# One factor moved out of the inverse sums, one copy moved to another engine, and a new order for the drain of an attention and feed-forward kernel

## Chip, cores and metric

The kernel runs on one core of a Trainium2 chip. The metric is the device time of one execution in microseconds (us). TensorE is PE, VectorE DVE, ScalarE ACT, GpSimd POOL, and SyncE (SP) issues the transfers. Instructions of one engine run in order; engines wait for each other only through semaphores.

## What is computed

```python
def layer(x, weight_qkv, out_w, out_b, W_r, W_k, W_v, mu_r, mu_k):     # x: 4 x 2048 x 256
    x = x + layernorm(attention(layernorm(x)))
    x = x + layernorm(ffn(layernorm(x)))

def attention(x):
    q, k, v = split(x @ weight_qkv)        # two column bands of x in fp16, the rest in fp32
    s = softmax((q / sqrt(256)) @ k.T)
    return (s @ v) @ out_w.T + out_b

def ffn(x):
    x_prev = x shifted by one row, zero in the first row of each batch
    xr, xk = mu_r * x + (1 - mu_r) * x_prev, mu_k * x + (1 - mu_k) * x_prev
    return sigmoid(xr @ W_r.T) * (square(relu(xk @ W_k.T)) @ W_v.T)
```

The layer norms have no learned factors and an epsilon of 1e-5.

## The kernel before

The 8192 rows are worked on in H = 32 halves of 256 rows, 8 for each of the 4 batches (PER = 8, RT = 2 tiles of 128 rows in a half). A half has 8 score tiles of 128x512, and one score tile is a slot: SLOTS = 256. The loops of all five engines run over the slots, and a table of offsets says in which slot after its own first one a half gets each operation: values from slot 23, the attention rows at 33, their normalization at 34, the turned sum and the differences at 45, the mixes at 48 and 50, receptance at 53, keys at 54, feed at 58, the gated rows at 59, the store at 65. So about nine halves are under way at a time, and where several operations fall in a slot, the order of the if statements is their order on that engine. Every product is made in split precision: a value is stored as a high fp16 part and a low part (value minus high), and three matmuls replace one. PE multiplies, ACT makes the high parts, exponents and most normalizations, DVE and POOL the low parts.

The next batch is loaded, normalized, split and transposed while the current one is computed (PREP, every 12 slots, during halves 10 to 15 and 18 to 23, and in the start-up).

What the change touches:

- inverse_sums(h), DVE: the reciprocal of the row sums (L1019), then its product with top[OUT], the largest magnitude of the folded projection weights, by which these weights had been divided (L1021). attention(h) uses the product as the factor of the projected rows (L1030) and adds bias_row.
- att_rsqrt(h), POOL: variance plus eps (L508), power -0.5 (L512), and the shift for attention_norm(h) on ACT (L765).
- scales(), POOL, once, in slot 17: the small factors that depend on the weights.
- mix_in_sum(h), differences(h), carry(h), POOL, slot 45. The first adds the two transposed parts into xt (L568), which has 257 columns; the second subtracts neighbouring columns (L577); carry copies the last column to column 0 of the other xt buffer, 128x2 elements, or clears it at the end of a batch (L589, L587). It waits for the mixes of the half before.
- ACT in slots of the kind of 46: receptance (L792) and gate_norm (L811); then in the next slot attended_high (y_hi, L695) and squares (L799 to L804).

Other names in the rows: probs and p_lo (L994, L1010) are the scores copied from PSUM and the low part of the exponents; q_lo (L985) and y_lo (L1014) are low parts of the query and of the attended values; rvar and rrstd (L524, L526) belong to res_rsqrt; pvar, prstd and xs (L467, L470, L919) to the preparation of a batch; res (L552 on POOL, L1097 on DVE) is add_attention; xm_lo (L595, L1112) is split_low.

After the last slot each engine runs a list of calls written out by hand, the drain, in which helpers of the same name exist on DVE and on POOL (split_low, squares_low, add_attention, differences, finish) and on DVE and ACT (attention_norm, gate_norm), so that the list decides who does it. In the drain the transposition for the mix goes through PE (turn_mix_in, L1365) instead of a transfer.

Of the kernel before, what the change touches and what calls it, by code (L numbers as in the profile page):

```python
# [8 lines left out]
ALU = mybir.AluOpType  # L9
# [3 lines left out]
P = 128  # L13
BLK = 512
EPS = 1e-5
# [3 lines left out]
def sandwich(nc, x, w_qkv, out_w, out_b, w_r, w_k, w_v, mu_r, mu_k, out):  # L19
# [51 lines left out]
    DIFF = 45  # L71
    MIX = (48, 50)
# [23 lines left out]
    MIX_LEFT = H - 6  # L96
# [9 lines left out]
    with ctx:  # L106
# [19 lines left out]
        eps = sb("eps", [P, RT])  # L126
# [144 lines left out]
        scales_made = sem("scales_made"); feed_part_made = sem("feed_part_made"); sum_inverted = sem("sum_inverted")  # L271
# [67 lines left out]
        def _(sp):  # L339
# [112 lines left out]
        def _(pool):  # L452
            pool.memset(ident[:, :], 0.0).then_inc(ident_zero, 1)
            pool.memset(minus_half[:, :], -0.5).then_inc(consts_made, 1)
            pool.memset(eps[:, :], EPS).then_inc(consts_made, 1)
# [6 lines left out]
            pool.wait_ge(consts_made, 3)  # L462
# [9 lines left out]
            def scales():  # L472
# [6 lines left out]
                pool.wait_ge(inv_top_made, 1)  # L479
                pool.tensor_scalar(mix_shrink[:, 0:1], top[:, MU:MU + 1], 2.0 ** -MIX_EXP, 0.0, ALU.mult,  # L480
# [99 lines left out]
            def carry(h):  # L580
                if h >= TURN_LEFT:
                    pool.wait_ge(xt_made, h + 1)
                if h >= 1:
                    pool.wait_ge(mixed_made[0], h * HALVES)
                    pool.wait_ge(mixed_made[1], h * HALVES)
                if (h + 1) % PER == 0:
                    pool.memset(xt[:, (h + 1) % 2, :, 0:1], 0.0).then_inc(carried, 1)  # L587
                else:
                    pool.tensor_copy(xt[:, (h + 1) % 2, :, 0:1], xt[:, h % 2, :, ROWS:ROWS + 1]).then_inc(carried, 1)  # L589

# [33 lines left out]
            for k in range(SLOTS):  # L624
# [14 lines left out]
                if (h := at(k, DIFF)) is not None:  # L639
                    mix_in_sum(h)  # L640
                    differences(h)
                    carry(h)
# [9 lines left out]
            carry(H - 5)  # L652
            att_rsqrt(H - 4, H - 3)
            add_attention(H - 4)
            split_low(H - 5, 1)
            res_rsqrt(H - 4)
            split_low(H - 5, 0)
            att_rsqrt(H - 3, H - 2)
            carry(H - 4)
            differences(H - 4)  # L660
            gate_rsqrt(H - 7, 0)
            finish(H - 7)
            gate_rsqrt(H - 6, H - 6)
            add_attention(H - 3)
            att_rsqrt(H - 2, 0)
            res_rsqrt(H - 3)
            finish(H - 6)
            split_low(H - 4, 1)
            carry(H - 3)
            differences(H - 3)  # L670
            res_rsqrt(H - 2)
            gate_rsqrt(H - 5, 0)
            split_low(H - 3, 1)
            finish(H - 5)
            carry(H - 2)
            squares_low(H - 4)
            split_low(H - 3, 0)
            att_rsqrt(H - 1, 0)
            split_low(H - 2, 1)
# [6 lines left out]
            gate_rsqrt(H - 3, H - 5)  # L686
            finish(H - 3)
            gate_rsqrt(H - 2, H - 4)
# [4 lines left out]
        def _(act):  # L693
# [87 lines left out]

            def split_high(h, i):
# [43 lines left out]
            for k in range(SLOTS):  # L826
# [30 lines left out]

            mix_in_out(H - 5)
            exponents(H - 1, 1)
            split_high(H - 6, 0)  # L860
            split_high(H - 6, 1)
            probs_high(H - 1, 0)
            attention_norm(H - 4, H - 3)
            split_high(H - 5, 1)
            probs_high(H - 1, 1)
            attended_high(H - 3)
            split_high(H - 5, 0)
# [652 lines left out]
```

## Time and profile before

| | |
|---|---|
| three runs | 830.95, 833.72, 833.16 us; median 833.16 |
| profiled execution | 831.39 us |
| its span, first to last instruction | 829.6 us |
| busy share of PE, DVE, ACT, POOL | 94%, 92%, 61%, 58% |
| first score matmul, last slot, last feed | 23.5, 750, 820.9 us |

In a row of the timeline the first figure is the start in us from the first instruction, the second the duration, then engine, line of the kernel, operation, output and inputs with their shapes, and in brackets the idle time of the engine before it with what ended it. Durations of neighbouring instructions on an engine overlap a little, matmuls above all; from start to start one of 256 columns takes 0.109 us and one of 512 columns 0.215 us.

### The profile page before, as it was taken

The page shows a single profiled execution, that of the slowest core. Times are in us where ns is not written, and L with a number is a line of the kernel's source. Part 1 is how long each engine was busy: PE and PEld are TensorE (multiplying, and loading weights), DVE is VectorE, ACT ScalarE, POOL GpSimd, SP SyncE. Part 2 cuts the span into 40 slices and gives each one's busy share as a digit, 9 for nine tenths or more (in the row PEclk, how much of TensorE's full clock was granted, in tenths as well). Part 3 has the DMA queues.
Part 4 walks back from the last instruction along what each step waited for, and adds up shares of the span by engine and source line. Part 5 has one row for each costly group of instructions (what it writes and reads, how often), then busy time and mean ns, then how long its engine had stood idle before and what let it go on. Part 6 is the DMA issues. An engine that isn't in the chain of part 4 may idle for free.

```text
span 829.6 us, 16266 instructions
## 1 busy us (share of the span) xinstructions
PE 782.6 (94%) x5765; PEld 568.3 (69%) x5765; DVE 759.6 (92%) x1822; ACT 510.0 (61%) x631; POOL 479.8 (58%) x692
## 2 busy tenths in 40 slices
PE   4879999999999998999999998999999999998983
PEld 3436677777767775777776775777777777777872
DVE  5698989999999999999999999999999999899895
ACT  3375555676666665667656666666766667665453
POOL 2210255577656566576655766656776576567674
PEclk9999999999999999999999999999999999999998
DMA  7565777587757585756676755747767465458301
GB/s 183 115 152 109 152 170 142 122 160 141 155 87 160 124 175 118 146 132 119 158 127 152 151 132 119 160 90 160 140 140 141 105 113 115 108 122 185 83 26 52
DMA packets 365090, 108.69 MB, mean 131 GB/s; under 512 B 338768, under 2 KB 364752, under 8 KB 365008
## 3 DMA queue, kind: packets, MB, share of 16 engines
q1 hardware_dynamic: 365008, 107.64, 62.4%
q8 instruction: 46, 0.75, 0.4%
q14 instruction: 36, 0.29, 0.1%
HBM read 18.75 MB, written 8.39 MB: 33 GB/s over the span
## 4 chain that ended last, share of the span: by engine, by line
PE 61%; DVE 32%; issue 4%; POOL 1%; DMA 1%; SPq 1%; ACT 0%; DVEq 0%; POOLq 0%
DVE p_lo L1010 7%; DVE probs L994 6%; PE S L1308 5%; PE S L1309 5%; PE S L1310 5%; PE S L1312 5%; PE S L1311 5%; PE Y L1329 4%; PE Y L1332 4%; PE Y L1330 4%; PE Y L1331 4%; PE Y L1333 4%; PE M L1276 4%; PE M L1278 4%; PE M L1277 4%
## 5 line engine op out<-in xcount | busy, mean ns | idle before, releaser
L994 DVE TENSOR_SCALAR_CACHE_REDUCE probs<-S 128x512 f32<-128x512 f32 x256 | 172.9, 676 | 18.2 <-PE S L1312 18.2
L745 ACT ACTIVATE probs<-probs,exp_bias,kappa 128x2048 f32<-128x2048 f32 x64 | 134.0, 2093 | 82.7 <-DVE exp_bias L1005 82.0
L1010 DVE TENSOR_TENSOR p_lo<-probs,p_hi 128x2048 f16<-128x2048 f32 x64 | 175.1, 2736 | 2.0 <-ACT p_hi L695 1.9
L1329 PE MATMUL Y<-pt_hi,planes 128*128 128x256 f16 x496 | 135.4, 273 | 0.0
L1330 PE MATMUL Y<-pt_lo,planes 128*128 128x256 f16 x496 | 135.3, 273 | 0.0
L1331 PE MATMUL Y<-pt_hi,planes 128*128 128x256 f16 x496 | 135.3, 273 | 0.0
L1332 PE MATMUL Y<-pt_lo,planes 128*128 128x256 f16 x496 | 135.3, 273 | 0.0
L1333 PE MATMUL Y<-pt_hi,planes 128*128 128x256 f16 x496 | 135.3, 273 | 0.0
L695 ACT ACTIVATE p_hi<-probs 128x2048 f16<-128x2048 f32 x64 | 121.4, 1897 | 18.4 <-DMA pt_lo<-p_lo 18.3
L1308 PE MATMUL S<-turned,q_hi 128*128 128x512 f16 x256 | 97.8, 382 | 15.2 <-DVE q_lo L985 12.1
L1309 PE MATMUL S<-turned,q_lo 128*128 128x512 f16 x256 | 97.8, 382 | 0.0
L1310 PE MATMUL S<-turned,q_hi 128*128 128x512 f16 x256 | 97.6, 381 | 0.0
L1311 PE MATMUL S<-turned,q_hi 128*128 128x512 f16 x256 | 97.5, 381 | 0.0
L1312 PE MATMUL S<-turned,q_lo 128*128 128x512 f16 x256 | 97.5, 381 | 0.0
L1067 DVE SCALAR_TENSOR_TENSOR mixed<-diff,mu,xt 128x256 f32<-128x256 f32 x128 | 82.1, 684 | 3.2 <-POOL diff L577 2.5
L595 POOL TENSOR_TENSOR xm_lo<-mixed,xm_hi 128x512 f16<-128x512 f32 x59 | 74.2, 1258 | 0.9 <-ACT xm_hi L695 0.9
L1329 PEld LDWEIGHTS Y<-pt_hi,planes 128*128 128x128 f16 x496 | 48.6, 98 | 30.7 <-issue 0.3
L1330 PEld LDWEIGHTS Y<-pt_lo,planes 128*128 128x128 f16 x496 | 48.6, 98 | 30.7 <-issue 0.3
L765 ACT ACTIVATE att<-att,ashift,arstd 128x256 f32<-128x256 f32 x60 | 32.8, 593 | 58.1 <-POOL ashift L516 58.1
L534 POOL TENSOR_TENSOR gvar<-gmv,gate_eps 128x2 f32<-128x2 f32 x32 | 6.7, 211 | 105.0 <-DVE gmv L1087 105.0
L695 ACT ACTIVATE xm_hi<-mixed 128x512 f16<-128x512 f32 x64 | 39.7, 622 | 43.8 <-DVE mixed L1067 41.1
L508 POOL TENSOR_TENSOR avar<-amv,eps 128x2 f32<-128x2 f32 x32 | 6.6, 205 | 89.0 <-DVE amv L1043 89.0
(208 smaller groups left out, 2047.9 us busy)
## 6 DMA issues: line engine op xcount, KB each, us to landing
x_res<-in_L_attn_x SPq DMA_DIRECT2D x32, 256.0 KB, 3.1
out_x<-gate SPq DMA_DIRECT2D x32, 256.0 KB, 2.2
xs<-in_L_attn_x SPq DMA_DIRECT2D x28, 128.0 KB, 3.0
xs<-in_L_attn_x SPq DMA_DIRECT2D x14, 256.0 KB, 3.4
pt_hi<-p_hi SPq DMA_TRANSPOSE x62, 4.0
pt_lo<-p_lo SPq DMA_TRANSPOSE x62, 4.0
mxt<-mx SPq DMA_TRANSPOSE x27, 3.3
pt_hi<-in_L_attn_weight_qkv SPq DMA_DIRECT2D x3, 128.0 KB, 3.1
```

The source lines that it names most:

```text
L695: return act.activation(out_, in_, ACT.Copy, scale=scale)
L994: dve.tensor_scalar(probs[:, h % 2, t, c * BLK:(c + 1) * BLK], S[k % RING][:, :], 1.0, None, ALU.mult, ALU.max, accum_out=chunk_max[:, t, ...
L1010: dve.tensor_tensor(p_lo[:, t, :], probs[:, h % 2, t, :], p_hi[:, t, :], ALU.subtract).then_inc(p_lo_made, 1)
L1308: pe.matmul(to, q_hi[:, h % 2, 0, rows], low, start=True, stop=False)
L1309: pe.matmul(to, q_lo[:, h % 2, 0, rows], low, start=False, stop=False)
L1310: pe.matmul(to, q_hi[:, h % 2, 1, rows], high, start=False, stop=False)
L1311: pe.matmul(to, q_hi[:, h % 2, 1, rows], rest, start=False, stop=False)
L1329: pe.matmul(to[:, 0, :], low, p_h, start=first, stop=False, skip_group_check=True)
L1330: pe.matmul(to[:, 0, :], low, p_l, start=False, stop=final, skip_group_check=True)
L1331: pe.matmul(to[:, 1, :], high, p_h, start=False, stop=False, skip_group_check=True)
L1332: pe.matmul(to[:, 1, :], high, p_l, start=False, stop=False, skip_group_check=True)
L1333: mm = pe.matmul(to[:, 1, :], rest, p_h, start=False, stop=final, skip_group_check=True)
```

## The change

The factor top[OUT] leaves the inverse sums. The projected rows therefore carry no factor, and what is added to them is scaled instead, once, in scales(): bias_row is divided by top[OUT], and the epsilon of the attention norm by its square (att_eps in place of eps). carry(h) moves from POOL to ACT, to slot 46, ahead of receptance; it now always waits for xt. The drain lists of all five engines are reordered, and some helpers change the engine. The slot table is otherwise as it was.

```diff
+    CARRY = 46
-        eps = sb("eps", [P, RT])
+        att_part = sb("att_part", [P, 1])
+        att_eps = sb("att_eps", [P, RT])
@@ scales, POOL @@
                 pool.wait_ge(inv_top_made, 1)
+                pool.tensor_scalar(bias_row[:, :], bias_row[:, :], inv_top[:, OUT:OUT + 1], 0.0, ALU.mult,
+                                   ALU.add).then_inc(bias_scaled, 1)
+                pool.tensor_tensor(att_part[:, :], inv_top[:, OUT:OUT + 1], inv_top[:, OUT:OUT + 1],
+                                   ALU.mult).then_inc(att_part_made, 1)
+                pool.wait_ge(att_part_made, 1)
+                for t in range(RT):
+                    pool.tensor_scalar(att_eps[:, t:t + 1], att_part[:, :], EPS, 0.0, ALU.mult, ALU.add).then_inc(att_eps_made, 1)
@@ att_rsqrt, POOL @@
+                if h == 0:
+                    pool.wait_ge(att_eps_made, RT)
-                pool.tensor_tensor(avar[:, :], amv[:, :, 1], eps[:, :], ALU.add).then_inc(a_eps_added, 1)
+                pool.tensor_tensor(avar[:, :], amv[:, :, 1], att_eps[:, :], ALU.add).then_inc(a_eps_added, 1)
@@ slots, POOL: the call of carry(h) goes; slots, ACT, behind mix_high @@
+                if (h := at(k, CARRY)) is not None:
+                    carry(h)
@@ new on ACT @@
+            def carry(h):
+                act.wait_ge(xt_made, h + 1)
+                if h >= 1:
+                    act.wait_ge(mixed_made[0], h * HALVES)
+                    act.wait_ge(mixed_made[1], h * HALVES)
+                if (h + 1) % PER == 0:
+                    copy(xt[:, (h + 1) % 2, :, 0], zeros[:, :]).then_inc(carried, 1)
+                else:
+                    copy(xt[:, (h + 1) % 2, :, 0], xt[:, h % 2, :, ROWS]).then_inc(carried, 1)
@@ inverse_sums and attention, DVE @@
-                dve.reciprocal(inv_sum[:, h % 4, :], row_sum[:, h % 4, :]).then_inc(sum_inverted, 1)
-                dve.wait_ge(sum_inverted, h + 1)
-                dve.tensor_scalar(inv_sum[:, h % 4, :], inv_sum[:, h % 4, :], top[:, OUT:OUT + 1], None,
-                                  ALU.mult).then_inc(inv_made, 1)
+                dve.reciprocal(inv_sum[:, h % 4, :], row_sum[:, h % 4, :]).then_inc(inv_made, 1)
+                if h == 0:
+                    dve.wait_ge(bias_scaled, 1)
@@ drain, SP @@
             turn_high(H - 2, 1)
+            turn_low(H - 2, 1)
+            store(H - 8)
             load_residual(H - 3)
-            store(H - 8)
-            turn_low(H - 2, 1)
```

The new drain lists, beginning and tail, in the order of the calls (h of H-n written as n; the rest is reordered in the same manner):

```
PE    project_out 4, values 3 (1..2), turn_mix_in 5, feed 7, values 3 (2..7), mix_keys 6, values 3 (7..8), receptance 6,
      values 2 (0..3), project_out 3, values 2 (3..6), mix_keys 5, values 2 (6..8), feed 6, values 1 (0..1), project_out 2, ...
      values 1 (5..8), mix_keys 4, project_out 1, turn_mix_in 2, receptance 4, mix_keys 3, feed 4, receptance 3, feed 3,
      mix_keys 2, receptance 2, turn_mix_in 1, feed 2, mix_keys 1, receptance 1, feed 1
POOL  squares_low 7, att_rsqrt 4, split_low 6 (1), add_attention 4, gate_rsqrt 7, split_low 6 (0), res_rsqrt 4, ...
      att_rsqrt 1, split_low 3 (0), add_attention 1, squares_low 3, split_low 2 (0), res_rsqrt 1, gate_rsqrt 4, ...
ACT   exponents 1 (1), probs_high 1 (0), mix_in_out 5, split_high 6 (1), carry 5, attention_norm 4, probs_high 1 (1),
      split_high 6 (0), gate_norm 7, squares 6, attended_high 3, receptance 6, ...
DVE   inverse_sums 2, attention 4, inverse_sums 1, mix 6, gated 7, probs_low 1 (0), residual_stats 4, probs_low 1 (1),
      finish 7, squares_low 6, attended_low 3, mix_in 4, differences 5, ...
      attention 1, mix 3 (0), differences 2, attention_norm 1, mix 2, gated 4, residual_stats 1, split_low 2 (1),
      gated 4 statistics, gated 3, mix_in 1, gate_norm 4, statistics, differences 1, mix 1, split_low 1 (1), ...
```

On DVE two split_low 6, squares_low 5, gate_norm 7 and 5, attention_norm 2, add_attention 2 and 1 and split_low 1 (0) are gone; finish 7 and 6, attention_norm 3, split_low 4 (1) and 2 (1) and gate_norm 2 are new.

## Rows read from the trace of the kernel before

**Rows 1.** Section 1 of the page, busy time of each engine.
```profile
PE 782.6 (94%) x5765; PEld 568.3 (69%) x5765; DVE 759.6 (92%) x1822; ACT 510.0 (61%) x631; POOL 479.8 (58%) x692
```

**Rows 2.** Windows by stage: length, then busy us (instructions) of PE, weight loads, DVE, ACT, POOL.
```profile
217.90:317.00 99.10, 95.63 (x715) 69.30 (x714) 95.51 (x230) 61.84 (x77) 62.49 (x92) 1.00 0.72 146
...
419.00:517.00 98.00, 94.41 (x702) 67.98 (x699) 94.86 (x226) 60.59 (x76) 61.61 (x89) 1.00 0.69 138
...
517.00:750.30 233.30, 231.90 (x1740) 170.09 (x1740) 217.81 (x505) 154.23 (x190) 150.81 (x210) 1.00 0.61 128
...
794.80:829.60 34.80, 19.38 (x152) 14.96 (x150) 25.32 (x58) 14.80 (x25) 21.56 (x32) 0.89 0.12 39
```

**Rows 3.** Timeline of PE, first score matmuls of halves 9, 13, 14, 29, 30 (start us, us).
```profile
194.24 0.38 PE L1308 MATMUL S<-turned,q_hi 128*128 128x512 f16 x1
...
289.86 0.38 PE L1308 MATMUL S<-turned,q_hi 128*128 128x512 f16 x1
...
316.98 0.61 PE L1308 MATMUL S<-turned,q_hi 128*128 128x512 f16 x1 [2.63 <-DVE q_lo L985]
...
679.21 0.38 PE L1308 MATMUL S<-turned,q_hi 128*128 128x512 f16 x1
...
702.91 0.38 PE L1308 MATMUL S<-turned,q_hi 128*128 128x512 f16 x1
```

**Rows 4.** Timeline of POOL and DVE around L1021 in a steady half.
```profile
688.48 1.15 POOL L595 TENSOR_TENSOR xm_lo<-mixed,xm_hi 128x512 f16<-128x512 f32 x1
...
688.58 1.08 DVE L1021 TENSOR_SCALAR inv_sum<-inv_sum,top 128x2 f32<-128x2 f32 x1
...
690.72 0.69 DVE L994 TENSOR_SCALAR_CACHE_REDUCE probs<-S 128x512 f32<-128x512 f32 x1 [1.06 <-PE S L1312]
```

**Rows 5.** Windows after the long wait (the figure behind POOL is PEclk).
```profile
317.00:320.00 3.00, 3.00 (x10) 1.37 (x11) 3.00 (x3) 2.11 (x4) 1.89 (x3) 0.50 0.00 0
```

**Rows 6.** Chain of waits, one of the eight pieces of L1021 before 317 and 517.
```profile
302.54 1.08 DVE inv_sum L1021
```

**Rows 7.** Lines L1021 and L1019: duration ns min/median/max, first and last start.
```profile
L1021 DVE TENSOR_SCALAR inv_sum<-inv_sum,top x32: 228/1078/1082, 55.4 to 758.6; 128x2 f32<-128x2 f32 x32
...
L1019 DVE RECIPROCAL inv_sum<-row_sum x32: 153/158/164, 55.2 to 758.5; 128x2 f32<-128x2 f32 x32
```

**Rows 8.** Timeline of POOL and DVE in the start-up.
```profile
57.77 1.02 POOL L470 TENSOR_TENSOR prstd<-pvar,minus_half 128x4 f32<-128x4 f32 x1
...
59.68 2.28 DVE L1010 TENSOR_TENSOR p_lo<-probs,p_hi 128x2048 f16<-128x2048 f32 x1
62.48 0.41 DVE L919 TENSOR_SCALAR xs<-xs,pmv,prstd 128x256 f32<-128x256 f32 x1
```

**Rows 9.** Timeline of DVE and POOL around the carried column.
```profile
699.16 3.06 DVE L1010 TENSOR_TENSOR p_lo<-probs,p_hi 128x2048 f16<-128x2048 f32 x1
...
700.01 2.25 POOL L589 COPY xt<-xt 128x2 f32<-128x2 f32 x1
```

**Rows 10.** Timeline of POOL, ACT and DVE around slot 46 of that half.
```profile
697.65 1.15 POOL L568 TENSOR_TENSOR xt<-mxt 128x512 f32<-128x512 f16 x1
...
697.46 0.69 ACT L792 ACTIVATE rec<-M,rec_scale 128x512 f32<-128x512 f32 x1 [1.57 <-PE M L1278]
...
703.19 0.68 DVE L1014 SCALAR_TENSOR_TENSOR y_lo<-Y,y_hi 128x512 f16<-128x512 f32 x1
```

**Rows 11.** Timeline of PE and POOL in the drain's opening.
```profile
751.69 0.66 PE L1365 MATMUL M<-ident,att 128*128 128x128 f32 x4 [2.31 <-DVE att L1059]
...
759.45 3.34 POOL L552 TENSOR_TENSOR res<-x_res,att 128x256 f32<-128x256 f32 x2 [0.80 <-ACT att L765]
```

**Rows 12.** Timeline of DVE and PE in the drain's tail.
```profile
802.35 2.10 DVE L1134 TENSOR_SCALAR att<-att,amv,arstd 128x256 f32<-128x256 f32 x2
...
809.39 1.57 DVE L1141 TENSOR_SCALAR gate<-gate,gmv,grstd 128x256 f32<-128x256 f32 x2
...
820.89 0.28 PE L1276 MATMUL S<-wt_hi,sq_hi 128*128 128x256 f16 x1 [1.26 <-DVE sq_lo L1119]
```

More of the change, by code:

```diff
@@ L95, in sandwich @@
     LEFT = H - 8
-    MIX_LEFT = H - 6
     TURN_LEFT = H - 5
@@ L685, in _ @@
             finish(H - 4)
-            gate_rsqrt(H - 3, H - 5)
+            gate_rsqrt(H - 3, H - 3)
+            split_low(H - 1, 0)
             finish(H - 3)
-            gate_rsqrt(H - 2, H - 4)
+            gate_rsqrt(H - 2, 0)
             finish(H - 2)
@@ L1203, in _ @@
             inverse_sums(H - 2)
-            mix(H - 6, 0)
-            mix(H - 6, 1)
-            differences(H - 5)
             attention(H - 4)
             attention_stats(H - 4)
-            split_low(H - 6, 1)
+            inverse_sums(H - 1)
+            mix(H - 6, 1)
+            mix(H - 6, 0)
+            gated(H - 7)
+            gated_stats(H - 7)
+            probs_low(H - 1, 0)
+            residual_stats(H - 4)
+            probs_low(H - 1, 1)
+            finish(H - 7)
+            squares_low(H - 6)
@@ L1210, in _ @@
+            attended_low(H - 3)
+            mix_in(H - 4)
+            differences(H - 5)
             mix(H - 5, 1)
[L1211 to L1213 removed]
             mix(H - 5, 0)
[L1215 to L1218 removed]
             attention(H - 3)
             attention_stats(H - 3)
[L1221 to L1223 removed]
@@ L1224, in _ @@
-            squares_low(H - 6)
-            gated_stats(H - 7)
+            attention_norm(H - 3)
             attended_low(H - 2)
             gated(H - 6)
-            gate_norm(H - 7)
             gated_stats(H - 6)
+            residual_stats(H - 3)
             attention(H - 2)
             attention_stats(H - 2)
-            split_low(H - 4, 0)
-            residual_stats(H - 3)
-            attention_norm(H - 2)
-            squares_low(H - 5)
-            mix_in(H - 3)
-            add_attention(H - 2)
@@ L1238, in _ @@
-            residual_stats(H - 2)
-            gated(H - 5)
-            mix(H - 3, 1)
-            gated_stats(H - 5)
-            mix_in(H - 2)
-            mix(H - 3, 0)
-            gate_norm(H - 5)
-            attended_low(H - 1)
-            differences(H - 2)
-            mix(H - 2, 1)
+            finish(H - 6)
+            mix_in(H - 3)
+            gated(H - 5)
+            mix(H - 4, 1)
+            gated_stats(H - 5)
+            mix(H - 4, 0)
+            residual_stats(H - 2)
+            split_low(H - 4, 1)
@@ L1248, in _ @@
+            mix(H - 3, 1)
+            attended_low(H - 1)
+            mix_in(H - 2)
+            split_low(H - 4, 0)
             attention(H - 1)
             attention_stats(H - 1)
+            mix(H - 3, 0)
+            differences(H - 2)
+            attention_norm(H - 1)
+            mix(H - 2, 1)
             mix(H - 2, 0)
             gated(H - 4)
-            attention_norm(H - 1)
-            add_attention(H - 1)
             residual_stats(H - 1)
+            split_low(H - 2, 1)
             gated_stats(H - 4)
@@ L1267, in _ @@
             squares_low(H - 1)
+            gate_norm(H - 2)
             gated(H - 1)
```

140 lines of the change are left out of this document (61 added, 79 removed).

## The prediction, made before the changed kernel was run

> **What bounds the kernel now.** I read the page first: TensorE (PE) is busy 94% of the span, VectorE (DVE) 92%, ScalarE (ACT) and GpSimd (POOL) about 60% [rows 1]. Shares so close say only that the bound changes hands, so I went to the windows. From 517 to 750 us PE has work in 231.9 of 233.3 us; in two earlier stretches of about 99 us it stands still for some 3.5 us each, and DVE is at its fullest there; after 750 both have holes [rows 2]. Three stages, then.
>
> In the undisturbed bulk a half (8 score tiles) lasts 23.70 us, from one first score matmul to the next [rows 3]. That is all PE: 40 score matmuls 0.215 apart and 138 others 0.109 apart make 23.6. DVE waits there: after the 1.08 us scaling of the inverse sums (L1021) it sits idle 1.06 us until PE hands over a score tile [rows 4]. What is taken from DVE in such a half is worth nothing.
>
> The two disturbed stretches are those in which the next batch is normalized and split, work that DVE has on top. From half 9 to half 30 there are 508.67 us for 21 halves [rows 3]; at 23.70 each they would take 497.7. So 11.0 us are lost. The half that begins at 289.86 (half 13) takes 27.12: it ends in a wait of 2.63 us for q_lo, which DVE makes late, and after it PE runs at a granted clock of 0.50 (its 1.2 GHz level) for some 3 us [rows 3, 5]. The other stops are small waits for y_lo or for the gated rows. By stretch: 4.1 us of stops and 1.6 us of slow clock before and just after 317, 4.9 us of stops between 441 and 518, 0.4 elsewhere. The chain of waits, followed back from the q_lo at 316.98, runs on DVE without a break to 223.9, and from 517 to 419.3 likewise. Each of these two passages holds four L1021 of 1.08 us, as in [rows 6]; all 32 of them have a median of 1.078 us, but the first took 0.228 and the reciprocal ahead of them takes 0.158 [rows 7]. The long ones begin 0.1 us after POOL's xm_lo begins and end with it [rows 4]: DVE is held by POOL.
>
> **The change, part by part.**
>
> *Inverse sums.* L1021 and the hand-over before it go: 1.08 + 0.03 = 1.11 us a half. Between 224 and 317 four of them are on the path: 4.4 us, against 4.1 us of PE stops. The stops go whole, and with them the slow clock: 4.1 + 1.6 = 5.7. In the second stretch 4.4 of 4.9 goes. Bulk: -10.1 us. More than -11.0 can't be had there; the lower end is in the rival below (-5).
>
> *Start-up.* scales() on POOL gains a 128x256 multiplication (POOL's addition of two 128x256 operands takes 0.72 on the mean), one tiny product and two tiny columns at 0.19 each: 1.25 us with hand-overs. It shifts pvar at 57.49 and prstd (1.02 us) to an end of 60.04; DVE wants prstd at 62.48 [rows 8]. Hidden, as long as prstd starts ahead of the p_lo at 59.68; behind it, it ends at 62.9 and DVE is 0.5 late. Against that stands the L1021 of 0.23 on DVE's path. I take 0, bounds -0.2 and +0.6. The wait of the first attention for the bias comes some 30 us later.
>
> *Carried column.* POOL's copy of 128x2 takes 0.18 to 2.25 us, 28 of them. The long ones are issued while DVE's p_lo runs and end with it [rows 9]. The next POOL instruction, rvar, reads SBUF too and would stand in the same place: it starts when p_lo ends, as now. So POOL gains 0.2 us in a steady half and the path nothing. On ACT no row shows a copy of this size: the bounds are 0.19 (the accumulator read, the shortest ACT row) and 2.25 (POOL's worst, if ACT could be held alike); I take 0.25, since the two forms are alike in size with the first, and no ACT row of one form varies with what DVE and POOL do: p_hi takes 1.89 to 1.90 beside contended and free neighbours. Its wait is the larger point. In slot 46 it stands ahead of receptance, gate_norm, y_hi and the squares, and it waits for POOL's xt, which ends at 698.80; the receptance ran at 697.46. Worked out: carry to 699.1, rec 0.68, gate 1.08, y_hi 0.60, so y_hi ends at 701.5 instead of 700.2. DVE takes it at 703.19: slack 1.7 us, in the tightest half 0.8 [rows 10]. The squares end at 703.5 instead of 702.9, the exponent after them starts 0.2 late. Nothing on the path: 0.
>
> *Drain* (from 749.2, 80 us). PE is busy 61 us of it [rows 2], the rest are waits. By counts DVE loses nine helpers (two split_low, squares_low, two gate_norm, an attention_norm, two add_attention, the last split_low) and gets six shorter or uncontended ones: 11.5 us against 4.6. Three parts:
> (a) Opening. PE stands 2.47 us for the mix_in rows, then another 0.38 [rows 11]. The new order begins with project_out, whose y_lo ends at 750.07: a stop of 0.95. Gain 1.9. The new SP order has turn_low before the store and the load; nobody waits for it there. But receptance(H-6) now needs POOL's split_low(H-6, 0), behind att_rsqrt, split_low, add_attention(H-4) and gate_rsqrt. By summing rows POOL ends it at 762.5 if add_attention takes 1.4, and at 765.4 if both it and the split are held by the two p_lo as add_attention was at 759.45 (3.34 us [rows 11]). PE wants it at 762.2. A new stop of 0.3 to 3.2, I take 1.9: (a) gives 0.
> (b) To the end of the values of H-1 at 794.8. Beside those in (a) PE has six stops between 766 and 789, together 2.7 us (start to start beyond the 0.109 of a matmul); the largest, 1.09, stands ahead of feed(H-6), whose sq_lo DVE now makes some 10 us earlier. I take half: -1.3.
> (c) Tail, H-1's own chain. Its attention_norm took 2.10 for what is 0.74 where POOL is quiet, the addition on DVE 1.71 where POOL needs 1.41, and its differences waited behind gate_norm at 1.57 and statistics [rows 12]. -1.3 for the norm, -1.2 for the differences, 0 for the addition; +1.3 because mix_keys(H-4) now stands between the values and project_out (12 x 0.109). Sum -1.2. From the last feed at 820.89 to the end, 8.7 us, the order is the same.
> Drain -2.5. Bounds: summing the new order through with uncontended durations and no held POOL gives about -5, with the slow clock in the last keys also gone -6; with the 3.2 us stop and (b), (c) at nothing or contended anew, +2.
>
> Sum: 831.39 - 10.1 - 2.5 = 818.8 us for the profiled execution. It lay 1.8 under the median of 833.16 and 0.4 over the lowest run, so I put a median run at 820.
>
> **A rule beside the sum.** The rows show DVE's L1021 held until POOL's xm_lo ends, and nothing else about whom POOL would hold without it [rows 4]. The Trainium skill, "SBUF — State Buffer", section "Who interferes with whom", says that VectorE in a two-port mode, and a VectorE instruction with two SBUF inputs against a GpSimd one that reads SBUF, contend for a shared pair of ports as an exclusive lock, and that the issue order decides who blocks. Taken strictly it speaks against a full gain: L1021 is only where the lock is met first, and an instruction of that kind behind it may pay instead; the mechanism and its time are rival 1, from rows. By my sum the trace decides for the full gain in most of the eight places.
>
> **Rivals.**
> 1. *The lock moves on.* The 1.1 us reappears in the next DVE instruction that POOL can hold: p_lo, 3.06 us where a free one takes 2.28 [rows 8, 9], or the reciprocal itself. For it: such an instruction follows within 2.7 us. Against: what directly follows in the disturbed halves are statistics or a score tile from PSUM, and these have the same length everywhere; and POOL's next operations depend on these statistics and shift along. If half of it is lost, the bulk gives -5: 825. Chance 0.15.
> 2. *The drain gives back.* The receptance stop in full and a contended tail, +2: 823.5 profiled, 824.5. Chance 0.14.
> 3. *Slower: ACT's queue.* The carried copy costs ACT more than thought, so that y_hi is late and project_out with it. It decides from 1.7 us above my 0.25. At 2.25, held as POOL is, with POOL's xt late by another 0.5, each of 24 halves loses 0.8: 820 + 19 = 839. Chance 0.05.
> 4. *No change.* The freed DVE time meets a wait that the chain doesn't show and the drain is even: 833. Chance 0.04.
> The forecast itself, 0.62.
>
> **Numbers.** Two runs of this kernel differ by up to 0.3%, 2.5 us. Faster than that is everything up to 830.7: the forecast, rivals 1 and 2, 0.91; same 0.04; slower 0.05. Range 814 to 828: below, drain at -6 and a median no farther from the profiled run than before; above, rivals 1 and 2 together and a little more.
>
> **What would show it.** In the profile after: halves of 23.70 us throughout, no wait of PE for q_lo; no granted clock of 0.50 near 317; DVE busy some 35 us lower; POOL's rvar at about 2.2 us where the copy was; ACT's copy near 0.25 us; the last values ending some 11 us earlier in all, the tail after them 34.8 us or less. Wrong it would be if p_lo or xs takes over the 1.1 us, if y_hi's end moves behind DVE's call for it, or if PE stands more than 3 us before receptance(H-6).

## The result, and the profile after

The changed kernel takes 826.68 us (median of 4 runs, 825.84 to 827.55), the kernel before 833.02 in runs on the same chip: a ratio of 0.9928, interval 0.9908 to 0.9949. It is faster by 0.7%, inside the stated range; 6.3 us were gained where 13 were forecast. The profiled execution took 826.91 us, span 824.9.

Section 1 of the page after, against [rows 1]. DVE lost 33 us of work (some 35 were expected), PE none:
```profile
PE 784.6 (95%) x5765; PEld 570.5 (69%) x5765; DVE 726.2 (88%) x1786; ACT 512.3 (62%) x664; POOL 495.0 (60%) x668
```

Timeline of PE after, first score matmuls of halves 9, 13, 14 and 30, against [rows 3]. From half 9 to half 30 there are now 498.02 us where there were 508.67, and half 13 lasts 23.70 where it lasted 27.12:
```profile
196.36 0.38 PE L1317 MATMUL S<-turned,q_hi 128*128 128x512 f16 x1
...
291.30 0.38 PE L1317 MATMUL S<-turned,q_hi 128*128 128x512 f16 x1
315.00 0.38 PE L1317 MATMUL S<-turned,q_hi 128*128 128x512 f16 x1
...
694.38 0.38 PE L1317 MATMUL S<-turned,q_hi 128*128 128x512 f16 x1
```

Windows after: the two stretches of next-batch preparation, the rest of the bulk, and the tail, with the columns of [rows 2]. PE has work in every microsecond of the first three, at full clock, and DVE has 5.5 us to spare in each of the first two. In the tail DVE is busy 30.2 of 38.4 us:
```profile
219.00:315.00 96.00, 96.00 (x723) 70.53 (x722) 90.46 (x231) 63.17 (x82) 66.83 (x90) 1.00 0.77 149
420.00:516.00 96.00, 96.00 (x720) 70.12 (x718) 90.46 (x229) 64.10 (x84) 67.53 (x87) 1.00 0.75 142
516.00:739.40 223.40, 223.40 (x1678) 163.93 (x1676) 200.77 (x467) 146.16 (x191) 145.30 (x192) 1.00 0.67 126
...
786.50:824.90 38.40, 21.16 (x167) 16.03 (x164) 30.22 (x64) 17.21 (x30) 25.28 (x34) 0.89 0.11 35
```

Waits after: engine, line waited in, whom for, us in total, times, longest. PE's waits for q_lo were 12.1 us in 5 before, among them two of 2.63 in the bulk; three are left, of 0.3 to 2.5 us, all in the start-up. New is POOL's xm_lo:
```profile
PE S L1317 <- DVE q_lo L998: 5.0, 3, 2.5
...
PE M L1285 <- POOL xm_lo L594: 3.6, 2, 3.0
```

Split by starts of PE's matmuls, the profiled executions differ like this:

| stretch | before, us | after, us | change | predicted |
|---|---|---|---|---|
| start to first score matmul | 23.49 | 23.77 | +0.3 | 0 |
| from there to half 7 | 123.36 | 125.20 | +1.8 | 0 |
| halves 7 and 8 | 47.39 | 47.39 | 0 | 0 |
| halves 9 to 29 | 508.67 | 498.02 | -10.65 | -10.1 |
| half 30 to the last score matmul | 45.00 | 45.00 | 0 | 0 |
| last score matmul to the last values | 46.58 | 47.12 | +0.5 | -1.3 |
| from there to the end | 35.11 | 38.40 | +3.3 | -1.2 |

With 0.2 us more around the span that makes -4.5, where -12.6 was predicted for a profiled execution. The bulk came as said. The drain gave 3.8 back instead of bringing 2.5. In the windows from the last score matmul to the end DVE's busy time fell only from 66.7 to 63.4 us, by 3.3, where the prediction's counts had 6.9.

### The profile page after: what moved, and what is told of

Read it like the earlier page. It is cut to its first block, busy times and chain, and to the rows that moved or that the text cites. A ratio compares the mean times of both kernels' runs of the same rounds, so it can differ in the third digit from the quotient of the medians.

```text
span 824.9 us, 16241 instructions
## 1 busy us (share of the span) xinstructions
PE 784.6 (95%) x5765; PEld 570.5 (69%) x5765; DVE 726.2 (88%) x1786; ACT 512.3 (62%) x664; POOL 495.0 (60%) x668
## 4 chain that ended last, share of the span: by engine, by line
PE 86%; DVE 8%; issue 2%; POOL 1%; ACT 1%; DMA 1%; SPq 1%; DVEq 0%; POOLq 0%; ACTq 0%
PE S L1317 6%; PE S L1320 6%; PE S L1321 6%; PE S L1318 6%; PE S L1319 6%; PE Y L1338 6%; PE Y L1339 6%; PE Y L1340 6%; PE Y L1342 6%; PE Y L1341 6%; PE M L1285 6%; PE M L1287 6%; PE M L1286 6%; DVE mixed L1079 1%; DVE probs L1007 1%
## 5 line engine op out<-in xcount | busy, mean ns | idle before, releaser
L1007 DVE TENSOR_SCALAR_CACHE_REDUCE probs<-S 128x512 f32<-128x512 f32 x256 | 173.3, 678 | 38.4 <-PE S L1321 37.6
L1023 DVE TENSOR_TENSOR p_lo<-probs,p_hi 128x2048 f16<-128x2048 f32 x64 | 163.9, 2561 | 5.3 <-ACT p_hi L691 5.3
L594 POOL TENSOR_TENSOR xm_lo<-mixed,xm_hi 128x512 f16<-128x512 f32 x60 | 83.0, 1385 | 8.4 <-ACT xm_hi L691 8.4
L1079 DVE SCALAR_TENSOR_TENSOR mixed<-diff,mu,xt 128x256 f32<-128x256 f32 x128 | 79.3, 663 | 1.0 <-POOL diff L587 0.8
L569 POOL TENSOR_TENSOR mx<-att,mx 128x512 f16<-128x512 f32 x27 | 34.0, 1258 | 43.1 <-ACT mx L691 43.1
L562 POOL TENSOR_TENSOR res<-x_res,att 128x256 f32<-128x256 f32 x64 | 57.9, 924 | 2.5 <-ACT att L761 1.6
```

The source lines that it names most:

```text
L1007: dve.tensor_scalar(probs[:, h % 2, t, c * BLK:(c + 1) * BLK], S[k % RING][:, :], 1.0, None, ALU.mult, ALU.max, accum_out=chunk_max[:, t, ...
L1023: dve.tensor_tensor(p_lo[:, t, :], probs[:, h % 2, t, :], p_hi[:, t, :], ALU.subtract).then_inc(p_lo_made, 1)
```

## The experiments

Two theories stood at the outset. The first: the new drain lists themselves cost some 4 us, whoever copies the carried column and however the sums are made, and the start-up's 2 us belong to the single execution. The rival: the additions to the start-up and the copy on ACT cost the time, and the drain is late only because what reaches it is. The four kernels of the first group take the change apart.

**e1_old_drain**: the kernel after with all five drain lists of before (the carried column copied by POOL there, by ACT in the slots).

> The changed kernel's bulk and scales with the drain lists of the kernel before (POOL carries in the drain). If the new lists are what cost 3.8 us after the last score tile: about 822.5 us (833.0 less 10.6, the start-up within 1 us either way), the stretch from the last score tile to the end 81 to 82 us, values of H-1 ending about 47 us after the last score tile and the tail behind them 35 us. If the drain is slow because it is reached in another state (transfers, the carry on ACT, POOL's backlog), whatever its order: 826 to 827, that stretch near 85.

**e2_only_drain**: the kernel before with the new drain lists alone, ACT's carry only in them.

> The kernel before with the new drain lists alone (the carry on ACT only there). If the lists cost: 836 to 837 us, with the waits of PE for xm_lo near 3 us ahead of receptance(H-6) and the pair of mixes of H-2 beside POOL's addition near 3.5 us again. If they are harmless in themselves: 833.

**e3_only_inverse**: the kernel before with the edits to the inverse sums, the bias and the epsilon alone.

> The kernel before with the factor taken out of the inverse sums alone; carry on POOL, old drain lists. If L1021 held by POOL is the whole gain of the bulk: halves 9 to 30 in 498 us instead of 508.7, time 822 to 823. If the carry's move to ACT has a part in it: halves 9 to 30 in more than 500 us and 825 or more.

**e4_only_carry**: the kernel before with the carried column on ACT in the slots alone.

```diff
+    CARRY = 46
@@ slots, POOL @@
-                    carry(h)
@@ slots, ACT, behind mix_high @@
+                if (h := at(k, CARRY)) is not None:
+                    carry(h)
```

> The kernel before with the carried column copied by ACT in the slots alone. By my sum nothing: 833, POOL's rvar at about 2.2 us in the place of the copy, halves 9 to 30 in 508 to 509 us. If POOL's relief or ACT's wait for xt counts: more than 1 us either way, seen in halves 9 to 30.

All runs in one table. The ratio is against runs of the kernel before on the same chip (medians 831.43 to 832.48), with its interval; the last four columns are us of the profiled execution: start to half 7, halves 9 to 29, last score matmul to the last values, last project_out to the last feed.

| kernel | median, us | ratio | to half 7 | halves 9 to 29 | values | tail |
|---|---|---|---|---|---|---|
| before, profiled | | | 146.85 | 508.67 | 46.58 | 23.98 |
| after, profiled | | | 148.97 | 498.02 | 47.12 | 26.92 |
| e1_old_drain | 822.15 | 0.9880 (0.9861 to 0.9900) | 148.17 | 498.00 | 46.29 | 24.00 |
| e2_only_drain | 834.74 | 1.0029 (1.0016 to 1.0041) | 146.83 | 508.31 | 44.87 | 27.13 |
| e3_only_inverse | 823.29 | 0.9885 (0.9860 to 0.9909) | 148.65 | 498.47 | 46.95 | 22.73 |
| e4_only_carry | 834.63 | 1.0029 (1.0016 to 1.0042) | 149.23 | 510.77 | 46.62 | 23.96 |
| e5_tail_fix | 823.70 | 0.9901 (0.9879 to 0.9922) | 146.03 | 497.99 | 45.46 | 26.03 |
| e6_opening_fix | 826.61 | 0.9945 (0.9925 to 0.9965) | 148.72 | 497.96 | 47.05 | 26.84 |
| e7_both_fix | 826.91 | 0.9932 (0.9911 to 0.9953) | 150.00 | 497.98 | 47.16 | 26.03 |
| e8_invert_20 | 824.32 | 0.9897 (0.9876 to 0.9917) | 146.95 | 498.26 | 46.75 | 23.99 |
| e9_tail_dve | 824.19 | 0.9905 (0.9890 to 0.9921) | 147.98 | 497.94 | 47.12 | 26.12 |
| e10_project_first | 822.34 | 0.9877 (0.9858 to 0.9896) | 148.74 | 497.98 | 46.28 | 23.98 |
| e11_control_before | 833.51, one run | | 149.67 | 507.99 | 46.57 | 23.97 |
| e12_control_after | 826.76, one run | | 149.09 | 498.12 | 47.13 | 26.83 |
| e13_tail_queue | 824.75 | 0.9904 (0.9877 to 0.9931) | 148.75 | 498.04 | 47.13 | 25.44 |
| e14_all_fix | 823.00 | 0.9896 (0.9876 to 0.9917) | 148.54 | 498.00 | 45.03 | 25.44 |

What the first four say. The edit to the inverse sums alone is worth about 9 us (823.29). The new lists cost 4.5 us on top of it: 826.7 for the kernel after, 822.15 with the old ones (4.0 by the ratios, which compare on one chip). On the kernel before they cost 2.3, their tail 3.15 longer and the stretch ahead of it 1.7 shorter; that is less than the 3 to 4 expected. The copy on ACT, on its own, makes the kernel before 0.3% slower. The rival falls for the drain: with the old lists the time from the last score matmul to the end is 81.34 us, as before (81.69), although everything else of the change is in.

**The inverse sums: instruction or lock.** e8_invert_20 is the kernel before with one number changed: the sums are inverted two slots later. L1021 and its 32 products stay.

```diff
-    INVERT = 18
+    INVERT = 20
```

> The kernel before with one number changed: the inverse sums two slots later (20 for 18), all instructions kept. In slot 20 POOL runs only its short gate operations. If the cost of L1021 is the time for which POOL's xm_lo holds it, and not the instruction: its median falls from 1.08 us to 0.2 or 0.3, halves 9 to 30 take 499 to 501 us instead of 508.7, time near 824 without any of the other edits. If the instruction itself is slow or the hold is met there too: nothing moves, 833.

Line L1021 of e8 on DVE, with the columns of [rows 7]: the median falls from 1078 to 262 ns. The halves 9 to 29 take 498.26 us, as much as without the instruction (498.02 after, 498.47 in e3):
```profile
L1021 DVE TENSOR_SCALAR inv_sum<-inv_sum,top x32: 228/262/931, 62.4 to 748.5; 128x2 f32<-128x2 f32 x32
```
So the 10 us of the bulk were the hold by POOL's xm_lo, and not the work of the product. No semaphore stands behind this wait: here engines wait for each other not only through semaphores, as was said at the outset. The hold can be avoided by a better slot as well as by another algebra.

**The carried column.** Lines of the kernel after that touch it (count | busy us, mean ns | idle before). ACT's copy takes 0.20 us where 0.25 was taken, and the end of y_hi stays at least 1.96 us ahead of DVE's y_lo in halves 3 to 26 (2.86 before). POOL's rvar has a mean of 1465 ns where it was 464, and DVE's two products of mix_in (L1071) 806 where they were 650:
```profile
L1071 DVE TENSOR_SCALAR att<-res,rmv,rrstd 128x256 f32<-128x256 f32 x64 | 49.0, 806 | 0.0
L534 POOL TENSOR_SCALAR rvar<-rmv,mix_shrink 128x2 f32<-128x2 f32 x32 | 46.9, 1465 | 3.9 <-DVE rmv L1066 3.9
...
L691 ACT ACTIVATE xt<-xt 128x2 f32<-128x2 f32 x28 | 5.6, 201 | 48.1 <-POOL xt L578 48.1
```
The first was predicted (rvar stands where the copy stood and waits as long), the second was not. Timeline of POOL and DVE after, in a steady half, beside [rows 9]:
```profile
714.32 3.07 DVE L1023 TENSOR_TENSOR p_lo<-probs,p_hi 128x2048 f16<-128x2048 f32 x1
...
715.22 2.30 POOL L534 TENSOR_SCALAR rvar<-rmv,mix_shrink 128x2 f32<-128x2 f32 x1
...
718.28 1.42 POOL L608 TENSOR_TENSOR gate<-gate,res 128x256 f32<-128x256 f32 x2
...
718.96 2.05 DVE L1071 TENSOR_SCALAR att<-res,rmv,rrstd 128x256 f32<-128x256 f32 x2
...
719.65 1.21 POOL L601 TENSOR_TENSOR sq_lo<-square,sq_hi 128x512 f16<-128x512 f32 x1
```
Timeline of the same place in the kernel before:
```profile
703.27 1.50 POOL L609 TENSOR_TENSOR gate<-gate,res 128x256 f32<-128x256 f32 x2
...
703.79 1.14 DVE L1059 TENSOR_SCALAR att<-res,rmv,rrstd 128x256 f32<-128x256 f32 x2
...
704.74 1.21 POOL L602 TENSOR_TENSOR sq_lo<-square,sq_hi 128x512 f16<-128x512 f32 x1
```
POOL, one small operation shorter, reaches its addition 0.15 us and its sq_lo 0.25 us sooner against DVE's p_lo than before (718.28 less 714.32 is 3.96; before 703.27 less 699.16 was 4.11). DVE's first mix_in product now meets the second part of the addition (0.89 us instead of 0.40), and the second product finds sq_lo running and ends 0.15 us after it, at 721.0; before it had started ahead of sq_lo and ended 0.15 us after the addition. The pair takes 2.05 us instead of 1.14. This is so in 16 of the 32 halves; in the kernel before it is so in halves 8, 16 and 24 alone, the ones in which its own rvar was held for 2.26 us. In the thirteen others that makes 11.2 us of DVE, of which the mixes behind the pairs give 4.6 back (in the half shown 1.77 instead of 2.14). In the kernel after DVE has that to spare. In e4, where L1021 is still there, it has not; that this is what makes e4 slower is read from its trace, no run has the one without the other. Waits of e4:
```profile
PE S L1320 <- DVE q_lo L997: 12.6, 6, 2.7
```
Halves 10 and 18 take 0.85 and 1.68 us more there, each ending in a stop of PE for q_lo (0.78 and 1.59) that the kernel before does not have, and halves 9 to 29 take 510.77.

**The drain's tail.** The next group goes after it. Timeline of POOL, DVE and PE after:
```profile
795.34 1.68 DVE L1146 TENSOR_SCALAR att<-att,amv,arstd 128x256 f32<-128x256 f32 x2
796.86 1.60 POOL L562 TENSOR_TENSOR res<-x_res,att 128x256 f32<-128x256 f32 x2 [0.32 <-DVE att L1146]
796.94 3.50 DVE L1079 SCALAR_TENSOR_TENSOR mixed<-diff,mu,xt 128x256 f32<-128x256 f32 x4
798.43 1.33 POOL L601 TENSOR_TENSOR sq_lo<-square,sq_hi 128x512 f16<-128x512 f32 x1
...
800.96 0.74 DVE L1060 BATCH_NORM_STATS2 rst<-res 128x6 f32<-128x256 f32 x2
801.18 0.27 PE L1285 MATMUL S<-wt_hi,sq_hi 128*128 128x256 f16 x1 [3.10 <-DVE gate L1087]
801.87 0.25 DVE L1066 BATCH_NORM_AGGREGATE rmv<-rst 128x2 f32<-128x6 f32 x2 [0.17 <-DVE rst L1060]
...
803.22 0.71 POOL L536 TENSOR_TENSOR rrstd<-rvar,minus_half 128x2 f32<-128x2 f32 x1
```
The attention norm has come down from 2.10 to 1.68 us and POOL's addition is done at 798.46. But DVE goes into the four mixes of H-2 at 796.94, which take 3.50 us beside POOL's addition and sq_lo (four mixes of this shape take 1.67 in the tail before), then into the gated rows, and starts the statistics of the last half only at 800.96, 2.5 us after they could begin. PE meanwhile stands 3.1 us before feed(H-3) for the same gated rows. Three edits to the lists:

e5_tail_fix puts the urgent chain first on DVE:
```diff
@@ drain, DVE @@
-            mix(H - 2, 1)
-            mix(H - 2, 0)
             gated(H - 4)
             residual_stats(H - 1)
+            mix(H - 2, 1)
+            mix(H - 2, 0)
```


> The changed kernel; on DVE the gated rows of H-4 and the statistics of the last residual come ahead of the two mixes of H-2 instead of behind them. If this order costs the tail: the second half of the residual statistics ends about 2.8 us earlier, the stop of PE of 3.3 us before feed(H-3) goes to under 1, the stretch from the last project_out to the last feed falls from 26.9 to about 24 us, and the time to about 824. If the tail is set by POOL's work (addition, low parts) instead: that stretch stays above 26.

e9_tail_dve has the statistics and gated(H-4) ahead of the mixes too, and takes add_attention(H-1) back to DVE.

> The changed kernel; the last addition of attention goes back from POOL to DVE, with the residual's statistics right behind it and the gated rows and mixes of H-2 after them. If the tail is long because H-1's chain goes over POOL and stands behind the mixes of H-2: from the last project_out to the last feed 24 to 25 us (26.9 before, 26.0 with only the order changed), time 823 to 824. If the whole set of new tail places is at fault (who makes the low parts, the feeds' order): it stays at 26.

e13_tail_queue is e5 with POOL's part of the same chain moved:
```diff
@@ drain, POOL @@
-            split_low(H - 2, 0)
             res_rsqrt(H - 1)
+            split_low(H - 2, 0)
```


> The kernel of e5_tail_fix, and on POOL res_rsqrt(H-1) ahead of split_low(H-2, 0). If POOL's queue is the second cause of the long tail: rrstd begins about 10.5 us after the last project_out instead of 13.96, the stretch from there to the last feed falls from 26.0 to 23 to 24 us, and from the last score tile to the end 80 to 81 us; time about 821.5. If DVE's own queue between (gated rows, their statistics) holds the mix input instead: rrstd moves, the feed does not, 823.7.

The chain of the last half, counted from the first matmul of project_out(H-1), in us:

| step | before | after | e5 | e13 |
|---|---|---|---|---|
| attention norm starts (DVE) | 5.44 | 6.09 | 6.08 | 6.08 |
| addition starts | 7.45 | 7.61 | 7.60 | 7.61 |
| last aggregation of the row statistics starts | 10.00 | 12.62 | 9.67 | 9.68 |
| rrstd starts (POOL) | 10.70 | 13.97 | 13.96 | 10.65 |
| mix_in starts (DVE) | 11.83 | 15.36 | 14.71 | 13.96 |
| differences start | 15.11 | 17.81 | 18.41 | 16.56 |
| last feed | 23.98 | 26.92 | 26.03 | 25.44 |

The table reads as a row of queues. e5 brings the statistics forward by 3.0 us and PE's stop before feed(H-3) down from 3.26 to 1.54, but rrstd does not move: on POOL it stands behind split_low(H-2, 0). e13 brings rrstd forward by 3.3, but mix_in is only 1.4 earlier than in the kernel after (0.75 than in e5), now behind the mixes, a split, the statistics and the gated rows on DVE. Timeline of POOL and DVE of e13: rrstd is there at 800.5 and mix_in begins at 803.08.
```profile
799.77 0.75 POOL L536 TENSOR_TENSOR rrstd<-rvar,minus_half 128x2 f32<-128x2 f32 x1
...
803.08 0.73 DVE L1071 TENSOR_SCALAR att<-res,rmv,rrstd 128x256 f32<-128x256 f32 x2
```
Of the 2.9 us that the tail lost, DVE's order was 0.9 and POOL's 0.6. The addition on POOL was not seen to matter: e9, with the addition on DVE, has its aggregation 0.4 us earlier (9.28) and a tail of 26.12 where e5 has 26.03. But rrstd stands behind POOL's split in both (14.07 and 13.97), so that what the addition would be worth with e13's order is not shown.

Both e5 and e13 stay behind what was expected of them (a tail of 24 us and of 23 to 24). The medians move by more than the tails, 3.0 us for e5 and 2.5 for e9, and e13, whose tail is the shorter one, has a higher median (824.75) than e5 (823.70): the edits are sized here by their stretches, and that e5 came near its expected 824 says nothing for its mechanism.

**The opening.** Timeline of PE, POOL and DVE after:
```profile
748.50 2.26 DVE L1023 TENSOR_TENSOR p_lo<-probs,p_hi 128x2048 f16<-128x2048 f32 x1
748.91 2.87 POOL L594 TENSOR_TENSOR xm_lo<-mixed,xm_hi 128x512 f16<-128x512 f32 x1 [1.69 <-ACT xm_hi L691]
...
753.95 2.26 DVE L1023 TENSOR_TENSOR p_lo<-probs,p_hi 128x2048 f16<-128x2048 f32 x1
754.19 2.07 POOL L552 TENSOR_TENSOR gshift<-gminus,grstd 128x2 f32<-128x2 f32 x1
756.22 1.15 POOL L594 TENSOR_TENSOR xm_lo<-mixed,xm_hi 128x512 f16<-128x512 f32 x1
757.42 0.28 PE L1285 MATMUL M<-wt_hi,xm_hi 128*128 128x256 f16 x1 [3.01 <-POOL xm_lo L594]
```
Both p_lo hold POOL: one its split (2.87 us for what takes 1.15), one the 128x2 shift of the gate (2.07 for 0.19). The receptance of H-6 comes 3.17 us late. Window after it, PEclk the third figure from the end: the clock is at its 1.2 GHz level for much of it, behind the 3.01 us in which PE stood still, and matmuls of 256 columns are 0.213 us apart instead of 0.109, which costs another 1.65:
```profile
757.50:761.50 4.00, 4.00 (x24) 3.00 (x25) 2.61 (x7) 2.76 (x5) 1.23 (x2) 0.61 1.03 118
```
In e5 and e2 the same lists have the same stop, 3.17 and 3.22 us, and the clock stays at 1.00 after it; their stretch to the last values is 45.46 and 44.87 us against 47.12. Of the six profiled executions with this opening, four (after, e9, e12, e13) have the slow clock.

e6_opening_fix moves POOL's split of H-6 up:
```diff
@@ drain, POOL @@
-            gate_rsqrt(H - 7, H - 6)
             split_low(H - 6, 0)
+            gate_rsqrt(H - 7, H - 6)
```


> The changed kernel; on POOL split_low(H-6, 0) goes ahead of gate_rsqrt(H-7). If the stop of 3.2 us before receptance(H-6) comes from POOL's queue, its shift being held by DVE's p_lo: the stop falls below 0.5 us and with it the slow clock after it, the values of H-1 end 2 to 4 us earlier after the last score tile (47.1 now), minus about 1 for a later y_lo of H-3; time about 824. If the stop only moves to project_out(H-3) behind ACT's later squares: no gain.

> Both edits in one. If they are the two causes and independent: about 821.5, and the stretch from the last score tile to the end near 80 us, below the 81.3 of the old lists. If one hides the other: no better than the better of the two.

e7_both_fix is e5 and e6 together; at 826.91 us it is no better than e6 (826.61), and worse than e5. The stop before the receptance goes in both, and comes back at project_out(H-3), which now waits for y_lo. Timeline of PE, e6:
```profile
761.71 0.39 PE L1285 MATMUL M<-wt_hi,y_hi 128*128 128x256 f16 x1 [2.93 <-DVE y_lo L1027]
```
e14_all_fix is e13 with e6's edit, and with the high and low part of the attended values of H-3 moved ahead of what stood before them on ACT (gate_norm(H-7), squares) and on DVE (finish(H-7), squares_low(H-6)).

> e13's edits, e6's edit, and attended_high(H-3) ahead of gate_norm(H-7) on ACT, attended_low(H-3) ahead of finish(H-7) on DVE. If the stop of 3 us in the opening is a chain of two queues (POOL's low part, then ACT's and DVE's attended rows): both stops go under 1 us, values of H-1 end 43 to 44.5 us after the last score tile (45.5 without a slow clock in e5), and the time is 818 to 820. If a third wait takes its place: no better than e13.

There both stops are gone, smaller ones of 0.64 and 2.10 us have come, and the clock stays up: 45.03 us to the last values. In all it takes 823.00 us, where 818 to 820 was expected; the old lists take 822.15.

e10_project_first asks whether the new opening is worth having without the rest: e1 with project_out(H-4) ahead of mix_in's transposition on PE and the exponents ahead of mix_in's output on ACT.

```diff
@@ drain, PE (e1 as base) @@
-            turn_mix_in(H - 5)
             project_out(H - 4)
-            values(H - 3, 1, 5)
+            values(H - 3, 1, 2)
+            turn_mix_in(H - 5)
+            values(H - 3, 2, 5)
```


> The changed kernel with the drain lists of before, and of the new lists only the opening: project_out(H-4) and one unit of values ahead of turn_mix_in(H-5) on PE, the exponents ahead of mix_in_out on ACT. If the opening of the new lists is worth what I summed: values of H-1 end 1 to 2 us earlier after the last score tile than the 46.3 of the old lists, time 821. If DVE and not PE paces that stretch: within 0.5 us of the old lists, 822.

The stretch to the last values takes 46.28 us as against 46.29. PE's stop at its head is 0.91 instead of 2.34, but new ones come behind (1.07 for a split of DVE), and all of them up to the last values make 4.1 us in both: the wait is passed on.

**PE's time in the drain, split.** From the last score matmul to the last feed every kernel has the same 525 matmuls on PE, 57.6 us at full clock; the rest are stops (start to start more than 0.13 us beyond a matmul's own 0.109 or 0.215) and slow clock (0.06 to 0.13 beyond). In us of the profiled executions:

| | whole | stops | slow clock |
|---|---|---|---|
| before | 72.98 | 13.77 | 1.61 |
| e1, old lists | 72.72 | 13.32 | 1.87 |
| after | 76.79 | 16.40 | 2.80 |
| e12, after again | 76.53 | 17.34 | 1.64 |
| e2, new lists alone | 74.43 | 15.56 | 1.37 |
| e5 | 74.06 | 16.52 | 0 |
| e13 | 75.31 | 16.11 | 1.65 |
| e14 | 73.22 | 15.69 | 0 |

Under the new lists PE stands 1.8 to 4 us longer, and none of the mended ones comes down to the stops of the old. In the profiled executions e14 comes within 0.5 us of e1 only because its clock stayed up; its mean granted clock was 0.993 there and 0.984 to 0.991 in its five other runs (821.66 to 825.59 us). Up to the last values the stops are 4.37 before and 4.70 after, and the stretch is 12 matmuls (1.3 us) shorter, those of mix_keys(H-4), which now come behind it; the 2.3 others are lost after the last values.

**Controls.** Both kernels unchanged, one execution each.

> The kernel before once more, for its profile. If the slow clock after 51 and 65 us, seen in the changed kernel, is a matter of the single execution: it may be here too, first score of half 7 at 149 instead of 146.9 us, and the stop at 317 or 512 may or may not be followed by a granted clock of 0.50. If it belongs to the change: half 7 begins at 146.9 again.

> The changed kernel once more, for its profile. Halves 9 to 30 in 498 us and 26.9 us from the last project_out to the last feed again, whatever the clock does; the start of half 7 at 146.9 or near 149, and values of H-1 ending 45.3 to 47.2 us after the last score tile, according to whether a slow clock follows the waits.

e12 repeats the kernel after to 0.4 us in every stretch, the slow clock after the stop at 757.65 included. e11 differs from the kernel before in the start-up: half 7 begins at 149.67 where it began at 146.85. Window of the start-up, after and then before, PEclk as above:
```profile
52.00:54.00 2.00, 2.00 (x6) 0.73 (x5) 1.45 (x8) 0.84 (x1) 0.00 (x0) 0.50 1.03 197
```
```profile
52.00:54.00 2.00, 2.00 (x11) 0.94 (x10) 1.83 (x12) 1.27 (x1) 0.27 (x2) 1.00 1.12 252
```
The wait ahead of it, 2.26 us for q_lo, is in every execution. In before, e2, e5 and e8 the clock stays at 1.00 behind it and half 7 begins by 146.95; in the twelve others it falls to 0.50 and half 7 begins at 147.98 or later. e11 and e4 are among the late ones, though their start-up is the same instructions as that of the kernel before; e5 is the earliest, with the additions to scales() in it. By counts, one of the eleven executions with these additions is early, and three of the five without them: whether the additions make the late start more frequent is not settled by so few.

## Why the prediction was partly right

**Bulk, -10.1: right, -10.65.** The stops for q_lo in the bulk went whole, with the slow clock near 317 and the second stretch's 4.9 us but for some 0.2. I had put 4.4 of those 4.9. One size inside it was off: in e11 the stop of 2.79 us that ends at 319.79 (the one at 316.98 before) is not followed by a slow clock but by another stop of 0.71 for y_lo, so the slow clock's own price there was about 0.85, not 1.6. DVE was late anyway.

**Rival 1, the lock moves on: refuted for L1021, seen for the carried column.** p_lo and the reciprocal did not take over the 1.1 us (p_lo's mean went from 2.74 to 2.56 us); e8 shows the same with the product still there. The Trainium skill, "SBUF — State Buffer", section "Who interferes with whom", calls the pair of ports that VectorE and GpSimd share an exclusive lock and says that the issue order decides who blocks. The trace agrees: two slots later the same product takes 0.26 us instead of 1.08, and in the carry's place, where both engines keep their order, the hold goes from the copy's 2.25 us to rvar's 2.30.

**Start-up, 0: not decided.** prstd ends at 60.64, ahead of the 64.33 at which DVE takes it up, so the way that was feared is not the one. The +1.8 us to half 7 goes with a slow clock that comes and goes between executions of one program (before and e11), but was there in ten of the eleven with the additions.

**Carried column, 0: right for this kernel, for too narrow a reason.** I said that POOL gains 0.2 us and the path nothing. POOL's 0.15 us turned into 0.9 us of DVE's mix_in in twelve halves and 0.5 in one. It is hidden only because L1021 left with it; on its own the move costs 2 us (e4). Where I costed the edit at nothing I named what covers it on ACT, and did not look at what a POOL that runs earlier meets. ACT's side (rival 3) was right: the copy is short and y_hi kept 1.96 us.

**Drain, -2.5: wrong, +3.8.** This is the step that failed, and the bound of +2 with it. By its parts:

(a) The opening stops at PE are 0.91 where I had 0.95, and the new stop before the receptance is 3.17. I had given 0.3 to 3.2 and taken 1.9, a middle, although the row beside it (the addition held for 3.34, [rows 11]) was of the very kind and the two p_lo stood in the list. The size was off by 1.3, and behind it came a slow clock of some 1.7 us in four of six executions. I had counted what slow clock would go, none that might come. The 0.38 that I had put down as a second stop is none: in [rows 11] four transpositions stand in one row, and 751.69 to 752.18 is their own time. So the gain at the head was 1.56 and not 1.9, and (a) came to +1.6 where I had 0. A stand of more than 3 us before receptance(H-6) was my own sign of being wrong, and the trace has it.

(b) I had -1.3 from other stops up to the last values, half of six that made 2.7. Two of the six were transpositions of 0.38 again; the other four make 1.9. After, none of them is left and one of 0.62 before mix_keys(H-6) is new: -1.3 came, out of a smaller sum, which is luck in the size. The largest, 1.09 before feed(H-6), is gone as forecast. With the 3.17 the stops of the stretch come to 4.70 where they were 4.37. (a) and (b) together gave +0.3 (e2: -0.2) and not -1.3. The stretch is shorter in e5 and e2 because 12 matmuls left it. That is the counterpart of the +1.3 that I had charged to (c), and I never credited it.

(c) The tail, -2.5 without that +1.3: the stops behind the last values came out 2.3 us longer. The norm did shorten (2.10 to 1.68, not to the 0.74 I had taken), and so did the way from mix_in to the differences (3.28 to 2.45). What I left out is in the list printed above: between attention_norm(H-1) and the statistics of H-1, DVE has both mixes of H-2 and gated(H-4), and POOL has a split before res_rsqrt(H-1). I priced the instructions of the chain and not the queue between them, and I took uncontended figures just where an addition and a split of POOL run beside DVE.

Rival 2 (the drain gives back, +2, 824.5) is what happened, at nearly twice its size, and it had deserved more than 0.14. That the median lies inside the range all the same is no merit of the sum: the range was wide enough to hold rival 1 and rival 2 together.

**What stays open.** Even e13 and e14 have 2.3 and 1.9 us more stops than before. Some 1.7 us of PE work (16 matmuls more) now lie between project_out(H-1) and the last feed, and mixes are held by POOL there (2.49 us for 1.67); how much each of these is worth was not told apart. With the old lists the tail is 23.96 to 24.00 us in six executions and 22.73 in e3, and why is not known. What decides whether the clock drops after such a stop was not found: the same stop in the same lists went both ways.

The best versions are the old lists with the rest of the change, 822.15 us, and the same with project_out first, 822.34, which cannot be told apart; both beat the kernel after by 0.5%. But e3, the edit to the inverse sums alone, has 0.9885 (0.9860 to 0.9909) where they have 0.9880 and 0.9877, and e8, one number changed, 0.9897 (0.9876 to 0.9917): nothing here shows that the copy on ACT or any of the new lists adds to what the product's hold was worth.

## What to carry to other kernels

When a list of calls is reordered, follow the last chain through every queue it passes, engine by engine, and write down what stands between its steps; a helper made shorter is worth nothing if two others were put before it. An instruction that is long only because a neighbour holds it is a matter of place: try another slot before other algebra. And when an operation leaves an engine, look at what that engine now meets earlier: 0.15 us sooner on POOL cost 0.9 us on DVE in a dozen halves.

## What the runs showed of the hardware

All 28 of the 128x2 fp32 copies on ACT take 0.19 to 0.21 us in the kernel after, where on POOL they took 0.18 to 2.25. A POOL instruction on 128x2 elements took 2.07 us beside DVE's p_lo (0.19 alone), and DVE's product of 128x2 1.08 beside POOL's xm_lo (0.23 to 0.26 elsewhere): in these rows not the size of what is held sets the price, but what it meets. A stop of PE of 2.3 to 3.2 us is followed in some executions by 2 to 4 us at a granted clock of 0.50, which cost 1.7 us in the drain, and not in others; e2 and e5 have it neither in the start-up nor in the drain's opening. Runs of one kernel spread here by 1.0 us (e1) to 6.3 (e13), and a slow clock more or less is of that order.
